# Loading the output-projection weight in four pieces, each as soon as its buffer region is free

## The reference, cut to what matters

```python
# x: (8, 2048, 2048); HEADS = 16, HEAD_DIM = 128
def attn(x, w_qkv, w_out):
    q, k, v = split(x @ w_qkv)                       # 16 heads of 128
    scores = q @ k.T / sqrt(128), causal
    out = softmax(scores) @ v                        # (b, s, 2048)
    return out @ w_out                               # the output projection

def ffn(x, weight, lora_A, lora_B, router_w):
    base = x @ weight.T
    w = top-2 of softmax(x @ router_w.T), renormalised
    return base + 2.0 * sum over 8 experts of w_e * (x @ A_e.T) @ B_e.T

x = x + layernorm(attn(layernorm(x), ...))
x = x + layernorm(ffn(layernorm(x), ...))
```

## Time and profile before

| | us |
|---|---|
| two runs | 2079.87 and 2175.00, median 2127.43 |
| the profiled execution, its own time | 2080.27 |
| span of its slowest core (core 7), first to last instruction | 2078.7 |
| spans of its eight cores | 2070.1 to 2078.7 |
| PE matmul busy | 1610.0 (77%) |
| ACT, DVE busy | 699.3 (34%), 687.9 (33%) |

### The profile page before, as it was taken

One profiled execution on the slowest core, in us unless ns is written; L12 is line 12 of the kernel. 1 busy time (PEld: TensorE's weight loads), 2 busy tenths in 40 slices (PEclk: granted clock), 3 DMA queues, 4 the chain that ended last, 5 costly groups with the idle time before them and its releaser, 6 DMA issues.

```text
span 2078.7 us, 25743 instructions; the slowest of 8 cores (2070.1 to 2078.7 us)
## 1 busy us (share of the span) xinstructions
PE 1610.0 (77%) x9552; PEld 826.3 (40%) x9552; DVE 687.9 (33%) x1697; ACT 699.3 (34%) x977; POOL 42.1 (2%) x59
## 2 busy tenths in 40 slices
PE   1229988988898898889889889508999409888885
PEld 1124444444444444444444444303444204444442
DVE  4552233233323323322332332202433304455454
ACT  4440322222222232232222222401333404665664
POOL 0000000000000000000000000000000100000000
PEclk9999999999999999999999999558999759889988
DMA  8321022012202202210220200092222390111111
GB/s 183 122 81 19 13 31 31 8 24 31 31 1 31 32 1 31 31 22 10 31 31 1 31 1 1 0 143 59 82 82 82 81 142 33 50 41 56 47 42 61
DMA packets 48633, 95.07 MB, mean 46 GB/s; under 512 B 5248, under 2 KB 38144, under 8 KB 42368
## 3 DMA queue, kind: packets, MB, share of 16 engines
q0 software_dynamic: 46064, 76.58, 20.1%
q1 hardware_dynamic: 2448, 16.85, 2.4%
HBM read 119.67 MB, written 16.78 MB: 66 GB/s over the span
## 4 chain that ended last, share of the span: by engine, by line
PE 62%; DVE 14%; ACT 9%; issue 7%; another core or an unknown queue 6%; DVEq 1%; DMA 0%; ACTq 0%; POOL 0%; SPq 0%; POOLq 0%
PE P_qkv L293 33%; PE P_qkv L490 8%; PE P_e L574 5%; PE P_o L574 5%; DVE sst L151 5%; PE P_sc L415 5%; ACT expT L454 3%; DVE ost L823 2%; ACT xln L221 2%; ACT x2s L817 1%; PE P_b L730 1%; PE P_b L786 1%; PE P_sc L443 1%; DVE sff L795 1%
## 5 line engine op out<-in xcount | busy, mean ns | idle before, releaser
L293 PE MATMUL P_qkv<-A,wbf 128*128 128x512 bf16 x3072 | 717.8, 389 | 0.7 <-DVE A L243 0.7
L293 PEld LDWEIGHTS P_qkv<-A,wbf 128*128 128x128 bf16 x3072 | 307.9, 100 | 389.1 <-issue 46.4
L427 ACT ACTIVATE expT<-P_sc,cbuf 128x1024 bf16<-128x1024 f32 x192 | 213.7, 1113 | 579.0 <-PE P_sc L415 579.0
L730 PE MATMUL P_b<-A,x2T 128*128 128x512 bf16 x1024 | 229.6, 386 | 0.4 <-DVE sff L795 0.4
L454 ACT ACTIVATE expT<-P_sc,cbuf 128x512 bf16<-128x512 f32 (+3 forms) x256 | 123.8, 525 | 279.5 <-PE P_sc L443 275.8
L490 PE MATMUL P_qkv<-Vaug,expT 128*128 128x129 bf16 x2176 | 176.2, 234 | 39.3 <-DVE srcp L501 26.1
L490 PEld LDWEIGHTS P_qkv<-Vaug,expT 128*128 128x128 bf16 x2176 | 145.5, 104 | 63.6 <-issue 62.9
L574 PE MATMUL P_e<-wo_bf,A 128*128 128x512 bf16 x512 | 114.2, 385 | 57.3 <-DMA wo_bf<-w_out 57.3
L730 PEld LDWEIGHTS P_b<-A,x2T 128*128 128x128 bf16 x1024 | 101.3, 100 | 121.7 <-issue 7.9
L415 PE MATMUL P_sc<-Qbf,Kbf 128*128 128x512 bf16 x384 | 128.7, 420 | 12.2 <-ACT expT L427 12.2
L443 PE MATMUL P_sc<-Qbf,Kbf 128*128 128x512 bf16 (+3 forms) x256 | 68.5, 309 | 81.8 <-ACT expT L454 59.2
(11 more groups left out here) (80 smaller groups left out, 1239.7 us busy)
## 6 DMA issues: line engine op xcount, KB each, us to landing
wbf<-wqkv POOLq DMA_DIRECT2D x16, 1536.0 KB, 15.8
expT<-x SPq DMA_DIRECT2D x16, 1024.0 KB, 6.1
xio<-x POOLq DMA_DIRECT2D x16, 1024.0 KB, 6.3
out<-ost POOLq DMA_DIRECT2D x16, 1024.0 KB, 4.2
wo_bf<-w_out POOLq DMA_DIRECT2D x2, 4096.0 KB, 42.7
A<-weightT POOLq DMA_DIRECT2D x2, 4096.0 KB, 42.9
sat<-at POOLq DMA_DIRECT2D x1, 512.0 KB, 58.4
sbf<-bflat POOLq DMA_DIRECT2D x1, 512.0 KB, 63.0
```

Of the source, the lines that this page charges most:

```text
L293: _p=wpar, _b=bank: e.matmul(P_qkv[:, 512 * _b:512 * _b + 512], wbf[:, 6144 * _p + 384 * _c + 128 * _m: 6144 * _p + 384 * _c + 128 * _m + ...
L427: e.activation(expT[:, 512 * _i:512 * _i + 1024], P_sc[:, 0:1024], AF.Exp, bias=EBIAS, scale=1.0),
L730: e.matmul(P_b[:, 512 * _f:512 * _f + 512], x2T[:, 2048 * _p + 128 * _c: 2048 * _p + 128 * _c + 128], A2[:, 2048 * _c + 512 * _f: 2048 * _ ...
```

## The change

`w_out` is loaded by four DMAs in place of two, on the same queue, at the same place in the queue's order. Each waits for less than the end of attention, except the last:

- chunks 0 and 1 (over `xln`): for the last transpose of stage 1,
- chunks 2 to 7 (over `wbf`): for the PE counter's value at the start of head 15,
- chunks 8 to 13 (over `Qbf`, `Kbf`, `VTs`): for the last diagonal score of head 15, block 3,
- chunks 14 and 15 (over `att`, `Vaug`, `expT`): for the end of attention on all engines, as before.

The first matmul of stage 3 waits for all four. Three dictionary entries (`marks`) take the values of the PE counter at those places; they issue nothing.

```diff
             xlnT_dve = c["dve"].v
+            marks = {"ln1_pe": c["pe"].v}
...
             for h in range(H):
                 hb = h % 2
+                if h == H - 1:
+                    marks["wbf_pe"] = c["pe"].v
...
                         exp_done[i] = ev
                         B.sg([bank], c["act"], ev)
+                    if h == H - 1 and qb == 3:
+                        marks["qk_pe"] = c["pe"].v
                     for w in range(2):
...
-            for hh in range(2):
-                B.emit("gpsimd", lambda s, _h=hh: s.dma_start(
-                    out=wo_bf[:, 16384 * _h:16384 * _h + 16384]
+            wo_pieces = [(0, 2, [(c["pe"], marks["ln1_pe"])]),
+                         (2, 8, [(c["pe"], marks["wbf_pe"])]),
+                         (8, 14, [(c["pe"], marks["qk_pe"])]),
+                         (14, 16, scope_w)]
+            for c0, c1, wwts in wo_pieces:
+                B.emit("gpsimd", lambda s, _a=c0, _b=c1: s.dma_start(
+                    out=wo_bf[:, 2048 * _a:2048 * _b]
                     .rearrange("p (x f) -> p x f", f=2048),
-                    in_=w_out[1024 * _h:1024 * _h + 1024, :]
+                    in_=w_out[128 * _a:128 * _b, :]
                     .rearrange("(x p) f -> p x f", p=128)),
-                    waits=(scope_w if hh == 0 else []),
-                    inc=c["ld_wo"], inck=16)
+                    waits=wwts, inc=c["ld_wo"], inck=16)
             wo_all = c["ld_wo"].v
```

## The result

The changed kernel takes 2046.25 us (median of 9 runs, 2044.03 to 2047.53). The ratio to the kernel before is 0.9845, with a 95% interval of 0.9832 to 0.9858. The run that was profiled took 2048.29 us against 2080.27 us for that of before, 32.0 us less. In some runs, whatever the kernel, the cores of one die (four of the eight) show a lower granted clock and take over 1% longer; ratios and medians from here on leave them out, which the medians of before, 2127.43 us of the first two runs and 2100.47 us of eight, don't.

The account below looks back on a forecast made before the run. The `w_out` transfer between attention and the output projection was taken as the limit. Issue at 1347.0 plus 30.1 plus 0.15 starts the PE at 1377.25 instead of 1410.98: 2080.27 - 33.7 = 2046.5 us, range 2039 to 2059.

Parts of the forecast that it names:

- Four issues, splitting: POOL queue: two more issues cost at most 2.3 us of idle POOL, and a queued piece no start-up; priced at zero.
- Chunks 0 to 7 hidden: Under attention: chunks 0 and 1 land by about 1168 us, 2 to 7 by 1320, with 26 us of slack.
- Chunks 8 to 13 at 1347.0: After head 15's last diagonal score at 1346.50 us: issue at 1347.0 and not 1354.57, 7.6 us earlier.
- Eight chunks in 30.1 us: Last eight chunks of `w_out`, from an idle queue: issue to landing 30.1 us, at 1377.1; lower bound 26.2 us.
- The sum: Projection start moves from 1410.98 to 1377.25 us: 33.7 us gained, time 2046.5 us, ratio 0.984.
- The clock: First 64 projection matmuls: stay at about 16.3 us against 13.81 for the next; term 0 to +2.5 us of gain.
- Rival A: Third piece, end of attention: issued early but moves only when DVE is done; gain 26.1 us, 2054.1 us; chance 0.08.
- Rival B: Last eight chunks: smaller or scattered pieces move at the head weights' rate, 42.1 us; time 2058.6 us; chance 0.07.
- Rival C: Head 15: transfers under it slow its work; 2063.5 us at half the cancelling price, 2107 if work triples; chance 0.02.
- Rival D: POOL queue: early pieces are held, all 16 chunks start at 1347.0 at best; 7.6 us gained, 2072.7 us; chance 0.03.
- E: Last eight chunks: land in 22.2 us, 189 GB/s, so the gain is over 2%, 41.6 us; chance 0.05.
- within 2%: Whole kernel: change lies within the 2% taken as what a measurement can tell from no change; chance 0.90.

Follow-up runs that it names:

- experiment 1: Changed kernel's four pieces, but all wait for the end of attention, so only the splitting is left; 2078.96 us, ratio 1.0005 to the kernel before.
- experiment 5: Kernel before with its two loads of `w_out` in the other order, rows 1024 to 2047 first; 2079.53 us, one run.
- experiment 4: experiment 3 with separate waits for the late chunks and the first projection tile taking early chunks first; 2022.72 us, ratio 0.9732.
- experiment 2: Changed kernel, but chunks 8 to 13 wait for the end of attention like the last piece; 2054.21 us, ratio 0.9877.
- experiment 6: Changed kernel, but chunks 2 to 7 are loaded twice under head 15; 2048.41 us, ratio 0.9855.
- experiment 3: Changed kernel in seven finer pieces, only chunks 9, 11, 14 and 15 issued after the last score; 2034.87 us, ratio 0.9787.

## Why the prediction was right or wrong

**What bounds the kernel; where the gain comes from.** Right. The block behind the load moved as one piece, and nothing downstream took it back.

**Four issues, splitting.** Right at zero: experiment 1, ratio 1.0005. The issues take 0.70 to 0.85 us each.

**Chunks 0 to 7 hidden.** Right. Issued at 1144.42 and 1296.15, where I had 1144.6 and 1297. On core 1 the first piece landed 18.7 us after its issue, at 1163, and the second 21.3 us after its own, at 1317.5, with 29 us of slack; I had 1168, 22.6 and 26.

**Chunks 8 to 13 at 1347.0.** Right: 1346.87.

**Eight chunks in 30.1 us.** Right on core 1: from 1346.87 to the first matmul at 1377.48 are 30.6 us, against the 30.25 of the sum. The eight cores have 27.6 to 31.7, mean 29.8. The choice of 30.1 over 26.2 rested on the load into an idle queue being the slower one, whichever rows it moves; experiment 5 shows it.

**The sum.** 33.7 us forecast, 32.0 measured between the two profiled executions, and 2046.5 against a median of 2046.25. Part of that closeness is luck: the same eight chunks differ by 4 us between cores, and it is the slowest core that counts. The 1.7 us between 33.7 and 32.0 are mostly not in the part that the sum worked out: on the slowest core the projection begins 33.5 us earlier (1410.98 and 1377.48). But the load of a part of stage 4's weight (`sbf`) took 64.5 us from issue to landing on core 1, where it took 63.0 on core 7 before, and the first matmuls of stage 4 wait for it. That load takes 56.6 to 64.5 us on the cores of the changed kernel, so which core is the slowest is partly decided there.

**The clock.** Right: the first 64 matmuls still take 15.2 to 16.9 us on the eight cores (15.3 to 16.9 before). The 2.5 us that the prediction left on the table are real: experiment 4 collects 2.4.

**Rival A**, transfer held back by DVE: 2054.1 us. Not seen. Experiment 2 is what it would have looked like (2054.21), and the changed kernel is 8 us faster. Nor does the third piece start later than a load with DVE at rest. On the eight cores its first 2 us after the issue carry 0 to 33 GB/s and the next two 139 on average; in the kernel before, issued when DVE had done, 0 to 33 and 117. On core 1 it is moving at 110 GB/s while DVE is busy 1.92 of 4 us:

```profile
1348.00:1352.00 4.00, 4.00 (x49) 4.00 (x47) 1.92 (x9) 0.00 (x0) 0.00 (x0) 0.65 0.75 110
```

What the Trainium skill (SBUF — State Buffer, "SBUF: two separate sides") tells of DVE shutting GpSimd out has no visible cost in this stretch. **Rival B**, the head weights' rate: 2058.6, not seen. **Rival C**, slowed work: not seen in experiment 6, where head 15 is as long as before to 0.01 us on seven cores of eight. **Rival D** is excluded by POOL's rows, **E** by the stall that is left.

**What was wrong: how much can be told from no change.** The step that failed is the sentence that about 2% is what a measurement of this kernel can tell, and the 0.90 set on "within 2%" with it. The stall, the wait, the overlap and the size were right; this step is where a real gain was set down as if it could not be told from none. My own sum said 1.6%, and the measured interval, 0.9832 to 0.9858, is far from 1: it is about 0.13%, or 2.7 us, to either side. The kernels are told apart by much less than 2%: experiment 1, with no gain, has 0.9995 to 1.0016, and experiment 2, 8 us behind the changed kernel, has 0.9862 to 0.9893, which does not touch the changed kernel's. That the time would lie within 2% was right, the reading of it as near no change was not. I should have said: almost surely faster, by less than 2%.

**What the prediction missed:** the first tile could be started before the whole weight is there. It took "starts when the load ends" as given, and reckoned only with how early the load ends. It also says nothing of the stall of 60.8 us at the start of stage 4, which is still there in the page of the changed kernel, ended by a load of stage 4; whether its loads can be moved forward in the same way was not tried.

```profile
L719 PE MATMUL P_x<-srt,x2T 128*128 128x8 bf16 x256 | 31.9, 202 | 60.8 <-DMA sbf<-bflat 60.8
```

## What to carry to other kernels

A load that waits for the end of a stage because its buffer lies on top of that stage's memory is not one wait but many: ask for each part of the buffer who reads the memory below last, and issue it there. Then the stall is the time of only those bytes that come free last, and if the first consumer also takes the early parts first, with its own wait for each late part, even these hide under it, and here the clock of TensorE was kept too. The steps took off 25.5 us of stall (the parts free before the last head), 6.9 (the part free at the last score), 12.3 (finer parts) and the last 11.0 with 2.4 us of slow matmuls (waits chunk by chunk).

## What the runs showed of the hardware that was not expected

A load into an idle queue pays for its start. Two chunks (1 MB as stored) took 9.3 us, eight took 29.5: so 3.4 us a chunk and about 2.5 us for the start, and a load that stands queued behind another pays less (25.2 us for eight). Most of the start is time in which little moves. Of the kernel before, the mean over the eight cores in steps of 2 us from the issue on is 16, 117, 198 and 162 GB/s, then 137 to 156 for 8 us, then 161 to 168; the rows below are of its core 7, issue at 1354.57 (columns as in experiment 3). Why was not tried.

```profile
1352.00:1356.00 4.00, 0.91 (x10) 0.50 (x7) 1.34 (x8) 0.00 (x0) 1.43 (x2) 1.00 0.01 4
1356.00:1360.00 4.00, 0.00 (x0) 0.00 (x0) 0.00 (x0) 0.00 (x0) 0.87 (x2) 0.72 0.89 130
1372.00:1376.00 4.00, 0.00 (x0) 0.00 (x0) 0.00 (x0) 0.00 (x0) 0.00 (x0) 0.50 1.02 166
```

Head 15 has two lengths: from V transposes to the last score 49.76 us on most cores, and 48.07 to 48.09 on one of eight before, three after, two in experiment 2, four in experiment 4 and none in experiment 6. Core 0 below has the short one and a higher granted clock. These are 12 us stretches of the changed kernel, core 0 (48.07 us) and then core 1 (49.77 us); the clock is third from the end.

```profile
1308.00:1320.00 12.00, 6.76 (x40) 3.91 (x40) 3.17 (x14) 5.23 (x7) 0.00 (x0) 0.64 1.03 167
```

```profile
1308.00:1320.00 12.00, 7.97 (x40) 3.92 (x40) 3.18 (x14) 4.32 (x7) 0.00 (x0) 0.50 0.76 116
```

The same 40 matmuls take 6.76 us on the one and 7.97 on the other. The lengths differ by 1.7 us, 1.2 of them in these 40 matmuls. Why one core is granted the higher clock and another is not was not tried.
